# A decoder layer with a mixture of experts: two chunks of the shared expert's second half ahead of the expert blocks, six register loads inside them

## The chip, the core and the metric

The kernel runs on one core of a Trainium2 chip. Its engines are PE (TensorE), DVE (VectorE), ACT (ScalarE), POOL (GpSimd) and SP (SyncE, which here only issues DMAs). Each engine works its own instructions in order, and semaphores tie them together. The metric is the device time of one launch in microseconds (us).

## What is computed

One decoder layer on 8 sequences of 128 tokens with 256 features: self-attention, cross-attention, then a feed-forward part. The change touches only that last part:

```python
shared = _silu_and_mul(x @ shared_gate_up_w.T) @ shared_down_w.T      # 704 hidden features
shared = shared * jax.nn.sigmoid(x @ sgate_w.T)
router_logits = x @ gate_w.T                                          # 16 experts
topk_w, topk_ids = jax.lax.top_k(jax.nn.softmax(router_logits), TOP_K)   # TOP_K = 4
def body(acc, ew):
    w13_e, w2_e, e = ew
    coef = jnp.sum(jnp.where(topk_ids == e, topk_w, 0.0), axis=-1)
    h = _silu_and_mul(x @ w13_e.T)                                    # 176 hidden features
    return acc + (h @ w2_e.T) * coef[:, None], None
out = shared + sparse_out
```

The result is added to x.

## The kernel before, in words

Every engine's program is written out by hand; nothing is scheduled by a planner. After the attention the feed-forward part runs in three stages.

**First shared half.** The shared expert works on 1024 tokens in two halves of 512. Its 704 hidden features are cut into SC = 6 chunks, so there are chunks 0 to 5 for the first half and 6 to 11 for the second. Each chunk is one `rows_of(n)` on PE (12 matmuls into two banks: first the gate part, then the up part), a Silu on ACT (`gate`, L735), a product on DVE (`gated`, which writes `hid`, L1179), a rounded copy on ACT (`high_hidden`, `hid_h`, L742), the remainder on DVE (`low_hidden`, `hid_l`, L1184) and one `down(n)` on PE (6 matmuls into `ps_y`). All shared matmuls stand on one line, L1453. Buffers of `silu`, `hid`, `hid_h` and `hid_l` are double, by n % 2. After `down(5)` the sum is copied out (`y_t`, ACT `take_y` L747 and DVE `finish` L1190), transposed by `turn_rows` (PE L1641) and added to x by `add_shared` (DVE L1198).

**Expert blocks.** The tokens were scattered by expert into `x_slots` in DRAM (POOL L543). NBLK = 40 blocks of 128 rows follow, each with 64 rows of one expert ("even") and 64 of another ("odd"). POOL gathers a block's rows (`xb`, L605), PE transposes them (`turn_block`, L1703), ACT copies the result (`take_rows_t`, `xbt`, L781), PE multiplies by the expert's weights (`block_up`, L1713 and L1715), ACT and DVE make the hidden rows (`sg` L789, `hb` L1252), PE transposes them (`turn_hidden`, L1725), ACT copies (`hbt`, L796), PE multiplies (`block_down`, L1735 and L1737), DVE scales (`take_block`, `yb`, L1259) and POOL scatters to `y_picks` (L597). ACT also copies the odd expert's weights aside (`copy_up`, `w13_odd`, shown as `w_odd<-w`, L810). Which expert a block has is read from seven packed words (six blocks each). ACT reads its seven with register loads at L800 before its first `copy_up`; PE reads its seven at L1683, between `turn_rows` and `turn_block(0)`, and unpacks a block's number with `unpack` (L1690 to L1692).

**Second shared half.** After the blocks PE runs chunks 6 to 11 with `rows_of` one chunk ahead of `down`. Meanwhile the picked rows come back (`yg`, eight DMAs by SP, L455), and DVE adds them up in 24 steps (`combine`, L1288, L1290, L1292: three per sequence), dealt between the chunks' products. Then `finish(1)`, `turn_rows(1, ...)`, the four last additions (L1311) and the stores of x.

An instruction whose semaphore is not there yet stops everything behind it on its engine.

Of the kernel before, what the change touches and what calls it, by code (L numbers as in the profile page):

```python
# [17 lines left out]
B, T, D = 8, 128, 256  # L18
# [10 lines left out]
NE, HE, HS = 16, 176, 704  # L29
SC = -(-HS // 128)  # L30
# [26 lines left out]
WARM = (13, 3, 22, 3)  # L57


def decoder_layer(nc, x_in, ctx_in, ctxt_in, wqkv_in, bqkv_in, wo_in, bo_in, rope_in, masks_in, gate_in,  # L60
                  w13_in, w2_in, shared_in, ident_in, iota_in, tri_in, upto_in, picks_in, dump_in, packs_in, out):
    ctx = ExitStack()
    with ctx:
# [558 lines left out]
        def _(act):  # L622
# [147 lines left out]
            for n in range(3, SC):  # L770
                high_hidden(n)
                if n + 1 < SC:
                    gate(n + 1)
            take_y(0)

# [54 lines left out]
            gate(SC)  # L830
            for n in range(SC, 2 * SC):
                high_hidden(n)
                if n + 1 < 2 * SC:
                    gate(n + 1)
# [4 lines left out]
        def _(dve):  # L839
# [402 lines left out]
            dve.memset(hb[:, :, HE:D], 0.0).then_inc(hb_padded, 1)  # L1242
            finish(0)
            for pair in range(2):
                add_shared(0, pair)

# [52 lines left out]
            gated(SC)  # L1299
            for n in range(SC, 2 * SC):  # L1300
                low_hidden(n)
                if n + 1 < 2 * SC:
                    gated(n + 1)
                combine(5 * (n - SC), min(5 * (n - SC) + 5, 3 * B))
            finish(1)
            for pair in range(2):
                m = 2 + pair
                dve.wait_ge(rows_turned, m + 1)
                for i in range(2):
                    b = 2 * m + i  # L1310
                    dve.scalar_tensor_tensor(x2[:, b, :], ps_rows[pair][:, D * i:D * i + D], sig[:, b:b + 1], x2[:, b, :],  # L1311
                                             ALU.mult, ALU.add).then_inc(x_out_ready, 1)
# [3 lines left out]
        def _(pe):  # L1316
# [361 lines left out]
            block_table()  # L1678
            down(5)
            pe.wait_ge(table_ready, 2)  # L1680
            for pair in range(2):
                turn_rows(0, pair)
            packed = [pe.value_load(words[0:1, i:i + 1], min_val=0, max_val=NE ** PACK - 1) for i in range(WORDS)]  # L1683
# [9 lines left out]

            unpack(0)
# [46 lines left out]
            pe.wait_ge(hid_ready, SC)  # L1741
# [7 lines left out]
            for n in range(NBLK):  # L1749
                if n + 1 < NBLK:  # L1750
                    block_up(n + 1)
                if n + 2 < NBLK:
                    unpack(n + 2)
# [9 lines left out]
            rows_of(SC)  # L1763
            pe.wait_ge(hbt_ready, NBLK)
            for n in range(SC, 2 * SC):
                if n + 1 < 2 * SC:
                    rows_of(n + 1)
                down(n)
            pe.wait_ge(yb_ready, NBLK)
# [81 lines left out]
```

## Time and profile before

| | |
|---|---|
| median of 3 runs | 402.47 us (400.6 to 404.37) |
| profiled execution, device time | 401.02 us |
| its span, first to last instruction | 399.2 us |
| mean granted TensorE clock | 0.952 |
| PE busy | 340.4 us (85%) |
| PE weight loads busy | 214.2 us (54%) |
| DVE busy | 228.8 us (57%) |
| ACT busy | 207.0 us (52%) |
| POOL busy | 178.2 us (45%) |

Times in the rows are us from the start of the span. Shares of busy time are averages over stages: the attention runs to about 190, the first shared half to about 222, the blocks from about 227 to 365, and the rest is the second shared half. A granted clock of 1.00 is TensorE at 2.4 GHz, 0.50 is 1.2 GHz.

### The profile page before, as it was taken

What the parts mean: (1) busy time and instruction counts of PE and PEld (TensorE: products, weight loads), DVE (VectorE), ACT (ScalarE), POOL (GpSimd) and SP (SyncE); (2) the same over time, 40 slices, a digit from 0 to 9 for tenths busy, and PEclk for the clock granted to TensorE, in tenths of its full rate; (3) what the DMA queues carried; (4) which work ended last, traced back from release to release, by engine and by line L of the source; (5) the groups of instructions that cost most, each with busy time, mean ns of one, the idle gap of its engine ahead of it and who ended that gap; (6) DMA issues with size and microseconds to landing.
All of it is one profiled execution on the core that took longest, in us unless ns stands there. A gap on an engine that the chain in (4) does not pass through costs nothing.

```text
span 399.2 us, 7934 instructions
## 1 busy us (share of the span) xinstructions
PE 340.4 (85%) x2362; PEld 214.2 (54%) x2378; DVE 228.8 (57%) x688; ACT 207.0 (52%) x557; POOL 178.2 (45%) x212
## 2 busy tenths in 40 slices
PE   6988799999999986679699497888878978989993
PEld 2445376767667653567487243444443433446772
DVE  3286579889898797734356242433333423343884
ACT  1265578897898668553152264545354535452321
POOL 5481314354443434572475335555645555643000
PEclk9899699999999999958989799999989999999999
DMA  6997987779698661121492425545535544553931
GB/s 227 317 296 246 383 242 186 226 192 315 191 265 238 181 182 54 62 90 57 160 398 71 148 68 163 151 147 152 185 114 162 160 136 151 164 161 100 351 123 53
DMA packets 41747, 72.54 MB, mean 182 GB/s; under 512 B 5346, under 2 KB 29042, under 8 KB 40562
## 3 DMA queue, kind: packets, MB, share of 16 engines
q1 hardware_dynamic: 35490, 56.08, 45.8%
q0 software_dynamic: 5376, 15.13, 11.3%
q10 hardware_dynamic: 848, 0.92, 0.7%
q8 instruction: 17, 0.28, 0.3%
q14 instruction: 16, 0.13, 0.1%
HBM read 40.58 MB, written 31.53 MB: 181 GB/s over the span
## 4 chain that ended last, share of the span: by engine, by line
PE 44%; DVE 15%; issue 13%; ACT 9%; POOL 7%; another core or an unknown queue 6%; DMA 4%; ACTq 0%; POOLq 0%; DVEq 0%; SPq 0%
PE bank L1713 10%; ACT probs L650 6%; PE bank L1453 6%; PE bank L1735 5%; PE bank L1375 3%; DVE neg_max L911 3%; POOL x_slots L543 3%; PE bank L1725 3%; PE bank L1367 2%; PE bank L1331 2%; PE bank L1362 2%; PE bank L1423 2%; PE bank L1703 2%; PE bank L1396 2%
## 5 line engine op out<-in xcount | busy, mean ns | idle before, releaser
L650 ACT ACTIVATE probs<-bank,neg_max 128x128 f32<-128x128 f32 x256 | 70.1, 416 | 8.0 <-DVE neg_max L911 8.0
L1713 PE MATMUL bank<-w,xbt 128*64 x160 | 56.7, 480 | 19.5 <-ACT xbt L781 11.4
L597 POOL DMA_INDIRECT y_picks<-yb,ids x40 | 39.4, 985 | 49.9 <-DVE yb L1259 40.2
L1715 PE MATMUL bank<-w_odd,xbt 128*64 128x352 f32 x160 | 56.8, 481 | 0.0
L1252 DVE TENSOR_TENSOR hb<-sg,bank 128x176 f32<-128x176 f32 x40 | 13.5, 338 | 73.6 <-ACT sg L789 37.9
L605 POOL DMA_INDIRECT xb<-x_slots,rows x40 | 38.6, 964 | 20.0 <-issue 7.3
L789 ACT ACTIVATE sg<-bank 128x176 f32<-128x176 f32 x40 | 12.7, 318 | 65.9 <-PE bank L1715 45.4
L1713 PEld LDWEIGHTS bank<-w,xbt 128*64 128x64 f32 x160 | 21.2, 141 | 44.0 <-issue 36.0
L543 POOL DMA_INDIRECT x_slots<-x,slots x32 | 32.2, 1007 | 27.7 <-DVE slots L1040 19.2
L911 DVE TENSOR_REDUCE neg_max<-bank 128x4 f32<-128x512 f32 x64 | 41.4, 682 | 5.0 <-PE bank L1367 4.9
L1737 PE MATMUL bank<-w_odd,hbt 128*64 128x256 f32 x160 | 43.7, 397 | 0.0
L1735 PE MATMUL bank<-w,hbt 128*64 x160 | 43.7, 397 | 0.0
L1375 PE MATMUL bank<-ident,probs 128*128 128x128 f32 x256 | 38.4, 279 | 4.9 <-ACT probs L650 4.4
L1375 PEld LDWEIGHTS bank<-ident,probs 128*128 128x128 f32 x256 | 28.4, 141 | 12.1 <-ACT probs L650 11.7
L810 ACT ACTIVATE w_odd<-w 128x704 f32 x40 | 31.6, 793 | 4.3 <-issue 4.3
L1259 DVE TENSOR_SCALAR yb<-bank,offset 128x256 f32<-128x256 f32 x40 | 19.3, 484 | 15.6 <-PE bank L1737 12.9
L515 POOL TENSOR_TENSOR rstd<-ve,expo 128x1 f32<-128x1 f32 x16 | 9.3, 580 | 41.3 <-DVE ve L952 41.3
L1735 PEld LDWEIGHTS bank<-w,hbt 128*64 128x64 f32 x160 | 18.9, 138 | 13.0 <-issue 7.4
L917 DVE COPY probs_t<-bank 128x512 f32<-128x512 f32 x32 | 20.6, 682 | 5.1 <-PE bank L1375 5.0
L1715 PEld LDWEIGHTS bank<-w_odd,xbt 128*64 128x64 f32 x160 | 21.2, 141 | 0.0
L486 POOL TENSOR_TENSOR turned<-qkv,rope 128x320 f32<-128x320 f32 x8 | 6.9, 866 | 31.7 <-DVE qkv L872 31.7
L657 ACT ACTIVATE probs_t<-bank 128x512 f32<-128x512 f32 x32 | 18.6, 646 | 4.5 <-PE bank L1375 4.5
(181 smaller groups left out, 735.6 us busy)
## 6 DMA issues: line engine op xcount, KB each, us to landing
x_slots<-zero_b SPq DMA_DIRECT2D x16, 1072.0 KB, 10.5
w_odd<-w_in_dram SPq DMA_DIRECT2D x40, 256.0 KB
w<-w_in_dram SPq DMA_DIRECT2D x4, 1408.0 KB, 12.2
w<-w_in_dram SPq DMA_DIRECT2D x4, 1024.0 KB
yg<-y_picks SPq DMA_DIRECT2D x8, 512.0 KB, 7.0
ktc<-keys_d SPq DMA_DIRECT2D x16, 192.0 KB, 3.3
sw_raw<-shared_in_dram SPq DMA_DIRECT2D x6, 384.0 KB, 3.6
keys_d<-ctxt_h SPq DMA_DIRECT2D x4, 512.0 KB, 6.5
```

The lines of the kernel that those rows point to most:

```text
L543: pool.indirect_dma_start(x_slots[:, :], bass.IndirectOffsetOnAxis(slots[:, TOPK * b + k:TOPK * b + k + 1], 0), x[:, b, :], None).then_inc ...
L597: pool.indirect_dma_start(y_picks[:, :], bass.IndirectOffsetOnAxis(ids[:, n:n + 1], 0), yb[:, n % RB, :], None).then_inc(yb_placed[n % RB] ...
L605: pool.indirect_dma_start(xb[:, n % RB, :], None, x_slots[:, :], bass.IndirectOffsetOnAxis(rows[:, n:n + 1], 0)).then_inc(xb_loaded[n % RB ...
L650: ins = act.activation(probs[:, g, j, :], ps_s[g][:, 128 * j:128 * j + 128], ACT.Exp, bias=neg_max[:, g, j:j + 1])
L810: act.activation(w13_odd[:, n % 2, :, :], w13[:, bass.ds(e, 1), :, :].rearrange("p e k n -> p (e k) n"), ACT.Copy).then_inc(w13_odd_ready, 1)
L911: dve.tensor_reduce(neg_max[:, g, :], ps_s[g].rearrange("p (j n) -> p j n", j=BLK), AX.X, ALU.max, negate=True).then_inc(max_ready[kind], 1)
L1375: ins = pe.transpose(ps_s[g][:, 128 * j:128 * j + 128], probs[:, g, j, :], ident[:, :])
L1453: ins = pe.matmul(outs, w, m, start=first and i == 0, stop=last and i == len(todo) - 1, skip_group_check=not (first and last))
L1713: pe.matmul(ps_gu[n % 2][0:ROWS, 0:GU], xbt[:, n % 2, k, 0:ROWS], w13[:, bass.ds(experts[n], 1), k, :].rearrange("p e n -> p (e n)"), star ...
L1715: ins = pe.matmul(ps_gu[n % 2][ROWS:128, 0:GU], xbt[:, n % 2, k, ROWS:128], w13_odd[:, n % 2, k, :], start=k == 0, stop=k == KC - 1)
L1735: pe.matmul(ps_yb[n % 2][0:ROWS, 0:D], hbt[:, n % 2, k, 0:ROWS], w2[:, bass.ds(experts[n], 1), k, :].rearrange("p e n -> p (e n)"), start= ...
L1737: ins = pe.matmul(ps_yb[n % 2][ROWS:128, 0:D], hbt[:, n % 2, k, ROWS:128], w2_odd[:, n % RW, k, :], start=k == 0, stop=k == KC - 1)
```

## The change

`AHEAD = 2`: chunks 6 and 7 of the shared expert (SC and SC + 1) get their `rows_of`, Silu, product, rounded copy and remainder before the blocks; their `down` stays behind the blocks. On PE, `rows_of(SC)` stands ahead of `down(5)` and `rows_of(SC + 1)` behind it. Behind the blocks PE alternates `down(n)` with `rows_of(n + 2)`. PE loads one packed word before the blocks and one more in each of the blocks 0, 5, 10, 15, 20 and 25, behind `block_up(n + 1)`. ACT keeps its seven loads in one piece. The 24 additions of routed rows on DVE are dealt as 5, 6, 6, 0 behind four chunks, then 3, `finish(1)`, and 4; before they were dealt as 5, 5, 5, 5, 4, 0 behind six. The first block's transposes on PE now wait for the product of chunk 7 (`hid_ready`, SC + AHEAD).

```diff
@@ ACT
             for n in range(3, SC):
                 high_hidden(n)
-                if n + 1 < SC:
-                    gate(n + 1)
+                gate(n + 1)
             take_y(0)
+            high_hidden(SC)
+            gate(SC + 1)
+            high_hidden(SC + 1)
...
-            gate(SC)
-            for n in range(SC, 2 * SC):
+            for n in range(SC + AHEAD, 2 * SC):
+                gate(n)
                 high_hidden(n)
-                if n + 1 < 2 * SC:
-                    gate(n + 1)
             take_y(1)
@@ DVE
+            gated(SC)
             finish(0)
+            low_hidden(SC)
+            gated(SC + 1)
             for pair in range(2):
                 add_shared(0, pair)
+            low_hidden(SC + 1)
...
             dve.wait_ge(rows_added, HB)
-            gated(SC)
-            for n in range(SC, 2 * SC):
+            done = 0
+            for n, more in zip(range(SC + AHEAD, 2 * SC), (5, 6, 6, 0)):
+                gated(n)
                 low_hidden(n)
-                if n + 1 < 2 * SC:
-                    gated(n + 1)
-                combine(5 * (n - SC), min(5 * (n - SC) + 5, 3 * B))
+                combine(done, done + more)
+                done += more
+            combine(done, done + 3)
             finish(1)
+            combine(done + 3, 3 * B)
@@ PE
             block_table()
+            rows_of(SC)
             down(5)
+            rows_of(SC + 1)
             pe.wait_ge(table_ready, 2)
             for pair in range(2):
                 turn_rows(0, pair)
-            packed = [pe.value_load(words[0:1, i:i + 1], min_val=0, max_val=NE ** PACK - 1) for i in range(WORDS)]
+            packed = []
+
+            def load_word():
+
+                w = len(packed)
+                if w < WORDS:
+                    packed.append(pe.value_load(words[0:1, w:w + 1], min_val=0, max_val=NE ** PACK - 1))
...
+            load_word()
             unpack(0)
             unpack(1)
...
-            pe.wait_ge(hid_ready, SC)
+            pe.wait_ge(hid_ready, SC + AHEAD)
...
             for n in range(NBLK):
                 if n + 1 < NBLK:
                     block_up(n + 1)
+                if n % (PACK - 1) == 0:
+                    load_word()
                 if n + 2 < NBLK:
                     unpack(n + 2)
...
-            rows_of(SC)
             pe.wait_ge(hbt_ready, NBLK)
             for n in range(SC, 2 * SC):
-                if n + 1 < 2 * SC:
-                    rows_of(n + 1)
                 down(n)
+                if n + AHEAD < 2 * SC:
+                    rows_of(n + AHEAD)
```

Where the instructions stand now. First ACT, from the last rounded copy of the first half to its first register loads. `silu` is the Silu, `hid_h` the rounded copy, `y_t` the shared sum, `words` the packed expert numbers. Before:

```order
L742 ACTIVATE hid_h<-hid 128x512 [waits down_done,hid_ready]
L747 ACTIVATE y_t<-bank 128x512 [waits down_done]
L800 TENSOR_LOAD words [waits table_ready]
L800 ISA x2
L800 TENSOR_LOAD words
```

and now:

```order
L743 ACTIVATE hid_h<-hid 128x512 [waits down_done,hid_ready]
L736 ACTIVATE silu<-bank 128x512 [waits hid_ready,up_psum]
L748 ACTIVATE y_t<-bank 128x512 [waits down_done]
L743 ACTIVATE hid_h<-hid 128x512 [waits down_done,hid_ready]
L736 ACTIVATE silu<-bank 128x512 [waits hid_ready,up_psum]
L743 ACTIVATE hid_h<-hid 128x512 [waits down_done,hid_ready]
L803 TENSOR_LOAD words [waits table_ready]
L803 ISA x2
```

Two Silus and two rounded copies stand ahead of the seven loads; the loads themselves, the first two `copy_up` and the first two `xbt` follow in the old order.

Then PE in block 0, from the second `block_up` to the transpose of the first hidden rows. `w_109` are the even expert's weights, `w_odd` the odd one's. Before:

```order
L1713 MATMUL bank<-w_109,xbt 64x352
L1715 MATMUL bank<-w_odd,xbt 64x352
L1690 REGISTER_ALU
L1691 REGISTER_ALU
L1725 MATMUL bank<-ident,hb 128x128 [waits hb_ready]
```

and now:

```order
L1729 MATMUL bank<-w_109,xbt 64x352
L1731 MATMUL bank<-w_odd,xbt 64x352
L1698 TENSOR_LOAD words
L1698 ISA x2
L1706 REGISTER_ALU
L1707 REGISTER_ALU
L1741 MATMUL bank<-ident,hb 128x128 [waits hb_ready]
```

One load and its two register instructions have come between a block's matmuls and the next transpose, in six of the forty blocks.

## Rows read from the trace of the kernel before

**Rows 1.** Busy time by stretch: engines, then PE clock, DMA share, GB/s.

```profile
219.60:225.90 6.30, 1.06 (x8) 0.86 (x8) 2.34 (x5) 2.05 (x3) 3.46 (x4) 0.86 0.63 193
...
231.30:365.00 133.70, 114.18 (x785) 57.08 (x781) 49.61 (x195) 62.91 (x154) 72.33 (x75) 0.99 0.49 147
```

**Rows 2.** Chain that ended last, 221 to 226 us: start, length, what.

```profile
221.52 3.54 DMA xb<-x_slots,rows
225.06 0.89 issue
```

**Rows 3.** Timeline, 217 to 228 us: start, length, engine, line, what [idle before].

```profile
217.89 0.50 PE L1453 MATMUL bank<-hid_h,sw_h 128*128 128x512 f32 x1
...
219.59 0.60 ACT L747 ACTIVATE y_t<-bank 128x512 f32<-128x512 f32 x1 [3.21 <-issue]
...
220.43 1.06 PE L1641 MATMUL bank<-ident,y_t 128*128 128x128 f32 x8 [0.88 <-DVE y_t L1190]
...
224.04 1.47 ACT L810 ACTIVATE w_odd<-w 128x704 f32 x2 [3.85 <-issue]
...
226.66 0.38 ACT L781 ACTIVATE xbt<-bank 128x256 f32<-128x256 f32 x1 [1.15 <-issue]
...
227.19 0.84 PE L1713 MATMUL bank<-w,xbt 128*64 x1
```

**Rows 4.** Register loads of ACT (L800) and PE (L1683): ns, first and last start.

```profile
L800 ACTq TENSOR_LOAD <-words x7: 273/275/651, 219.6 to 223.2; - x7
...
L1683 PEldq TENSOR_LOAD <-words x7: 301/304/495, 220.5 to 224.6; - x7
```

**Rows 5.** Timeline behind the blocks: one chunk of the second half.

```profile
364.94 0.73 PE L1453 MATMUL bank<-xth,sw_h 128*128 128x512 f32 x2
...
368.15 0.69 DVE L1179 TENSOR_TENSOR hid<-silu,bank 128x512 f32<-128x512 f32 x1 [2.61 <-PE bank L1453]
...
368.87 0.63 ACT L742 ACTIVATE hid_h<-hid 128x512 fp32r<-128x512 f32 x1 [1.64 <-DVE hid L1179]
...
369.53 0.69 DVE L1184 TENSOR_TENSOR hid_l<-hid,hid_h 128x512 fp32r<-128x512 f32 x1 [0.70 <-ACT hid_h L742]
...
370.51 0.40 PE L1453 MATMUL bank<-hid_h,sw_h 128*128 128x512 f32 x1
...
370.77 0.69 DVE L1179 TENSOR_TENSOR hid<-silu,bank 128x512 f32<-128x512 f32 x1 [0.54 <-PE bank L1453]
...
371.91 0.63 PE L1453 MATMUL bank<-xth,sw_h 128*128 128x512 f32 x2
```

**Rows 6.** Block 37 on PE: last register instruction of `unpack`, then the transpose.

```profile
L1692 PEldq MOVE  x1: 29/29/29, 357.5 to 357.5; - x1
...
L1725 PE MATMUL bank<-ident,hb x2: 273/300/328, 358.4 to 358.6; 128*128 128x128 f32 x2
```

**Rows 7.** Busy time by shorter stretches, columns as in rows 1.

```profile
199.80:204.00 4.20, 4.17 (x13) 3.34 (x14) 2.81 (x5) 2.65 (x6) 3.37 (x4) 0.59 1.01 422
...
230.00:231.00 1.00, 1.00 (x6) 0.48 (x4) 0.67 (x4) 0.70 (x2) 0.00 (x0) 0.51 0.00 0
```

**Rows 8.** Timeline of the second half's end.

```profile
372.20 0.69 DVE L1288 TENSOR_TENSOR yg<-yg 128x512 f32<-128x512 f32 x1 [0.74 <-DMA yg<-y_picks]
...
374.90 0.69 DVE L1184 TENSOR_TENSOR hid_l<-hid,hid_h 128x512 fp32r<-128x512 f32 x1
...
391.90 0.51 PE L1453 MATMUL bank<-hid_h,sw_h 128*128 128x512 f32 x1 [1.77 <-DVE hid_l L1184]
...
393.60 0.69 DVE L1190 COPY y_t<-bank 128x512 f32<-128x512 f32 x1 [1.76 <-PE bank L1453]
...
395.10 1.66 DVE L1311 SCALAR_TENSOR_TENSOR x<-bank,sig,x 128x256 f32<-128x256 f32 x4 [0.81 <-PE bank L1641]
```

**Rows 9.** Waits in the blocks, 226 to 364 us: us in total, times, longest.

```profile
ACT sg L789 <- PE bank L1715: 45.4, 33, 2.3
...
ACT sg L789 <- remote: 19.6, 6, 4.2
```

More of the change, by code:

```diff
@@ L57 @@
 WARM = (13, 3, 22, 3)
+AHEAD = 2
 def decoder_layer(nc, x_in, ctx_in, ctxt_in, wqkv_in, bqkv_in, wo_in, bo_in, rope_in, masks_in, gate_in,
```

## The prediction

> **What bounds the kernel now.** I read the busy time by stretch first. Of the places that the change touches it has a stretch of 6.3 us before the blocks in which PE is busy for only 1.06, and the blocks themselves (133.7 us, PE busy 114.2) [rows 1]. The change moves two chunks' worth of PE work from behind the blocks into the first stretch.
>
> Next the chain across the gap. It runs over the first gather (221.52, landed at 225.06) and 0.89 of issue to the first transposes on PE [rows 2]. So PE's hole belongs to a DMA, and PE work put there looks free. But the chain shows only the wait that ended last. The timeline shows a second one nearly as long on ACT: after `y_t` at 219.59 ACT does nothing until `copy_up` at 224.04, and its first `xbt` follows at 226.66; `block_up(0)` starts at 227.19 [rows 3]. The register loads fill that hole: seven on ACT with starts from 219.6 to 223.2, 0.6 each, and seven on PE from 220.5 to 224.6, (224.6 - 220.5) / 6 = 0.68 each [rows 4]. PE's loads begin while its `turn_rows` matmuls (220.43 for 1.06) still run, so a load needs PE's sequencer and not its array [rows 3, 4].
>
> ACT has little slack there: the two `copy_up` end at 224.04 + 1.47 = 225.51, `xbt` starts at 226.66. That is 1.15 us [rows 3].
>
> **Term 1, the start of the blocks.** Prices of a chunk come from behind the blocks: two `rows_of` take 364.94 to 370.51, so 2.78 each; a `down` takes 370.51 to 371.91, 1.40; the product of chunk 7 starts at 370.77, which is 3.05 after its `rows_of` (364.94 + 2.78 = 367.72); the rounded copy starts 368.87 - 368.15 = 0.72 after a product, the remainder 369.53 - 368.15 = 1.38 after it [rows 5].
>
> PE used to start `down(5)` at 217.89 [rows 3]. Now `rows_of(6)` runs from 217.89 to 220.67, `down(5)` to 222.07, `rows_of(7)` to 224.85. The product of chunk 7 starts at 222.07 + 3.05 = 225.12, its rounded copy on ACT at 225.84. DVE and ACT are free by then: `y_t` starts 1.70 after `down(5)` does (219.59 - 217.89), at 220.67 + 1.70 = 222.37, and chunk 6's rounded copy and remainder behind it end by 224.4.
>
> ACT's seven loads stand behind that rounded copy. Before, ACT's first `copy_up` came 224.04 - 219.59 = 4.45 after the activation ahead of the loads began; now it comes at 225.84 + 4.45 = 230.29. Two copies (1.47) bring `xbt(0)` to 231.76 instead of 226.66, and `block_up(0)` to 232.29. **That is +5.1 us**, though the gather lands at 225.06 as before. SP, POOL and their queues are passed by nothing, since they are not touched. PE's own six loads that leave this place save nothing, because ACT's seven end later than the one PE keeps.
>
> Bounds: not below +3.9 (4.45 counted without ACT's first slow load, 0.65 instead of 0.28, and 0.8 off the chunk), not above +6.0 if `y_t` pushes chunk 6 and 7 back by one ACT copy and one DVE copy more.
>
> **Term 2, TensorE's clock.** The granted clock fell during PE's idle, was still 0.51 between 230 and 231, and is 0.99 on the mean from 231.3 on [rows 1, 7]. Block matmuls from 227.19 to about 231.2 thus ran at 1.2 GHz, 4.0 us for what takes 2.0. Now PE idles from about 226.5 (both `turn_block` done) to 232.29, 5.8 us, longer than the idle before, so I expect the fall again. The fall before that one, from 199.8 to 204.0 with 0.59 on the mean, was shorter: 4.2 x (1 - 0.59) / 0.5 = 3.4 us at half speed [rows 7]. Ends: -2.0 if the clock never falls, +1.0 if it stays low 2 us longer. I take -0.5, since the transposes at least no longer run slow.
>
> **Term 3, loads in the blocks.** Six loads of 0.68 are 4.1 us if PE stands still for each. The order puts each behind a block's matmuls were dispatched. In block 37 the sequencer was through with `unpack` at 357.5 while the transpose behind it started at 358.4: PE's sequencer is 0.9 ahead of the array there [rows 6]. A load of 0.68 fits. So I take 0, upper end 4.1, lower end 0 (a load gives nothing back).
>
> The Trainium skill, in "DMA: Bandwidth & Descriptors", section on latency and other measured facts, gives a register load a floor of about 600 ns; it speaks against this edit, because six would be an estimated 3.6 if none were hidden. By the row above the sum has 0 for them.
>
> **Term 4, the end.** I count u from PE's first shared matmul behind the blocks (364.94). Before, the last additions begin at u = 395.10 - 364.94 = 30.16 and the span ends 4.1 after that [rows 5, 8]. Now PE does `down(6)` to 1.40, `rows_of(8)` to 4.18, `down(7)` to 5.58, `rows_of(9)` to 8.36, and is ready to be done with all ups at 16.7. DVE decides. Product of chunk 8 at 1.40 + 3.05 = 4.45, remainder done at 4.45 + 1.38 + 0.69 = 6.52. The picked rows arrive at 372.20, u = 7.26, since nothing in their chain is touched; five steps take 372.20 to 374.90, 2.7, so six take 3.2 [rows 8]. Then:
> - five steps to 9.9, chunk 9 (product to remainder 2.07) to 12.0,
> - six steps to 15.2, chunk 10 to 17.3,
> - six steps to 20.5, chunk 11 to 22.6,
> - `down(11)` on PE, 1.70 until its copy (391.90 to 393.60 [rows 8]), 24.3; three steps beside it,
> - `finish(1)` to 25.0, four steps to 27.1; the transposes end at 25.8 in their shade,
> - last additions from 27.1 instead of 30.16: **-3.1 us**.
> Bounds: -1.5 (if each chunk's copy on ACT costs DVE 0.4 more) to -4.0.
>
> **Sum.** 5.1 - 0.5 + 0 - 3.1 = +1.5. Against the profiled execution, 401.02, that is 402.5. The median of the runs shown, 402.47, lies 1.45 above that execution, so as a median I write 402.47 + 1.5 = 404.0.
>
> **Rivals.**
> - *The clock stays up* because PE works through the old hole. Against it: the new hole is longer. 402.47 + 5.1 - 2.0 - 3.1 = 402.5. Chance 0.14.
> - *The loads in the blocks show.* For it: ACT waits for PE's `block_up` 33 times, 45.4 us, so PE is what the blocks wait for [rows 9], and 0.9 ahead is not much. 402.47 + 1.5 + 4.1 = 408.1. It decides from about 2.6 us exposed, 0.4 per load. Chance 0.17.
> - *The rhythm of the blocks shifts.* Six waits of ACT for something that the trace can't name took 19.6 us [rows 9]; one more or one less is 3.3, so 400.7 or 407.3. The three runs of before already lie 3.8 apart. Chance 0.13, both signs.
> - *Faster: the end becomes PE's.* If the additions fit beside PE's work, the end is 4 x 2.78 + 6 x 1.40 = 19.5, then 0.3, 1.5 to the additions: 21.3 instead of 30.16, -8.9, and 402.47 + 5.1 - 0.5 - 8.9 = 398.2. It needs DVE to be idle less than my list has it, from u = 7.3 on; DVE's list is solid there. Chance 0.06.
> - My forecast: 0.50, its own range 402 to 406.
>
> **How the numbers follow.** About 1% (4.0 us, 398.4 to 406.5) is what a measurement of this kernel can tell from no change. Faster by more: 0.06 and a part of the rhythm, 0.09. Slower by more: 0.17, a part of the rhythm and the top of term 1, 0.23. Same: 0.68. The range goes from the rhythm's lower case, 400.4, to the exposed loads, 408.0.
>
> **What would show it.** Right: `copy_up` starts at about 230, `block_up(0)` at about 232.3, ACT's register loads begin right behind a `hid_h` at 225.8; the last block ends about 4.6 later than before; from there to the end of the span 3.1 less. Wrong: `block_up(0)` before 230 (term 1), the first PE transpose of hidden rows in blocks 0, 5, 10 later after `block_up` than in their neighbours (term 3), DVE waiting for PE again behind u = 10 (term 4).

## The result, and the profile after

| | before | after |
|---|---|---|
| median, five executions of each side by side | 400.6 us (396.39 to 404.37) | 405.3 us (403.41 to 411.7) |
| ratio, 95% interval | | 1.0172 [1.0097, 1.0247] |
| profiled execution | 401.02 us | 409.17 us |
| its span | 399.2 us | 407.2 us |
| mean granted TensorE clock | 0.952 | 0.937 |
| product of chunk 5 to `block_up(0)` | 12.50 us | 17.36 us |
| `block_up(0)` to `block_up(5)` | 15.52 us | 16.48 us |
| `block_up(5)` to the end of the last block | 122.29 us | 121.90 us |
| end of the last block to the last additions | 30.09 us | 30.62 us |

The changed kernel is 4.7 us slower by the medians. Twelve more executions of it on a chip that also ran the kernel before gave 400.24 against 395.66, a ratio of 1.0119 [1.0074, 1.0165]. So the change costs between 1 and 2%, nearer 1. All ratios here leave out executions more than 1.5% above the fastest of the same kernel.

Its profiled execution is not a typical one: its span is 8.0 us longer, and 2.04 of that lies ahead of everything the change touches (the product of chunk 5 on DVE starts at 216.74, before at 214.70). The last four lines of the table hold the other 6.0: +4.86, +0.96, -0.39, +0.53. I use such stages for all runs below, each taken from the starts of the same instructions in the timeline.

First the start of the blocks, from the timeline of the changed kernel (start, length, engine, line, what, and in brackets the idle time ahead and what ended it), then its register loads by line (ns, first and last start):

```profile
219.97 0.73 PE L1460 MATMUL bank<-xth,sw_h 128*128 128x512 f32 x2
...
222.83 0.40 PE L1460 MATMUL bank<-hid_h,sw_h 128*128 128x512 f32 x1
...
224.42 0.60 ACT L748 ACTIVATE y_t<-bank 128x512 f32<-128x512 f32 x1 [2.16 <-PE bank L1460]
...
227.94 0.63 ACT L743 ACTIVATE hid_h<-hid 128x512 fp32r<-128x512 f32 x1 [1.54 <-DVE hid L1180]
...
232.21 1.47 ACT L813 ACTIVATE w_odd<-w 128x704 f32 x2 [3.64 <-issue]
...
234.09 0.84 PE L1729 MATMUL bank<-w,xbt 128*64 x1 [4.70 <-ACT xbt L784]
```

```profile
L803 ACTq TENSOR_LOAD <-words x7: 272/275/471, 227.9 to 231.4; - x7
...
L1698 PEldq TENSOR_LOAD <-words x7: 297/308/493, 225.3 to 323.3; - x7
```

ACT's seven loads run from 227.9 on, behind the rounded copy of chunk 7, and leave ACT idle by the profile for 3.64. PE waits 4.70 for the `xbt` behind them. Before, the same wait on ACT stood right behind `y_t`, beside the gather [rows 3]. The second thing is the clock. Busy time by stretch of PE alone (length, PE busy, clock, DMA share, GB/s), first of the kernel before, then of the changed one:

```profile
223.00:224.00 1.00, 0.00 (x0) 1.00 0.84 272
224.00:225.00 1.00, 0.00 (x0) 0.58 0.89 266
```

```profile
232.00:233.00 1.00, 0.00 (x0) 1.00 0.00 0
233.00:234.00 1.00, 0.00 (x0) 0.66 0.02 8
...
239.00:240.00 1.00, 1.00 (x6) 0.50 0.00 0
240.00:241.00 1.00, 0.44 (x3) 0.92 0.47 116
```

In both kernels the clock fell to its lower level, 1.2 GHz, after PE had been idle (since 221.5 before, since 229.4 now), and stayed there for nearly 7 us (from about 224.2 to 231.0 [rows 7], and from 233.3 to 240.1). Before, 3.0 of these passed before `block_up(0)` at 227.19; now only 0.8 did, so 2.2 us more of block matmuls ran at half speed, an estimated 1.1; the stage is 0.96 longer.

Last the end of the changed kernel, where the picked rows `yg` come back. The last two lines are from the view of the DMAs between 376 and 385 us: `q8` holds instruction fetches, and the last number of the other line is the median time from issue to landing.

```profile
380.46 0.69 DVE L1293 TENSOR_TENSOR yg<-yg 128x512 f32<-128x512 f32 x1 [1.35 <-DMA yg<-y_picks]
...
383.85 0.69 DVE L1293 TENSOR_TENSOR yg<-yg 128x512 f32<-128x512 f32 x1 [1.78 <-DMA yg<-y_picks]
...
385.04 0.69 DVE L1180 TENSOR_TENSOR hid<-silu,bank 128x512 f32<-128x512 f32 x1
...
387.17 0.50 PE L1460 MATMUL bank<-hid_h,sw_h 128*128 128x512 f32 x1 [2.07 <-DVE hid_l L1185]
...
397.36 0.80 PE L1460 MATMUL bank<-hid_h,sw_h 128*128 128x512 f32 x1 [3.49 <-DVE hid_l L1185]
...
403.09 1.66 DVE L1318 SCALAR_TENSOR_TENSOR x<-bank,sig,x 128x256 f32<-128x256 f32 x4
```

```profile
q8 instruction: 1, 0.02, 1.0%
...
yg<-y_picks SPq DMA_DIRECT2D x8, 512.0 KB, 8.3
```

DVE's fourth addition waits 1.78 for the second block of rows, with the product of chunk 9 (385.04) queued behind it, and PE's `down(9)` behind that. The last `down` starts behind 3.49 of idle at half clock (0.80 for its first matmul, 0.50 at 387.17). Before, the second block of rows was taken 1.53 after the first (8.71 and 7.19 behind the last block); here 3.39 after it. "Behind the last block" means from the end of its last `block_down` here and below.

### The profile page after: what moved, and what is told of

Read it like the earlier page. It is cut to its first block, busy times and chain, and to the rows that moved or that the text cites. A ratio compares the mean times of both kernels' runs of the same rounds, so it can differ in the third digit from the quotient of the medians.

```text
span 407.2 us, 7933 instructions
## 1 busy us (share of the span) xinstructions
PE 343.3 (84%) x2362; PEld 217.9 (54%) x2378; DVE 227.9 (56%) x688; ACT 206.8 (51%) x557; POOL 178.6 (44%) x212
## 4 chain that ended last, share of the span: by engine, by line
PE 43%; DVE 15%; issue 12%; another core or an unknown queue 9%; ACT 9%; POOL 6%; DMA 3%; ACTq 1%; POOLq 0%; DVEq 0%; SPq 0%
PE bank L1460 10%; PE bank L1729 8%; ACT probs L651 5%; PE bank L1382 4%; DVE neg_max L912 3%; PE bank L1751 3%; PE bank L1338 2%; PE bank L1741 2%; PE bank L1374 2%; POOL x_slots L544 2%; DMA yg<-y_picks 2%; PE bank L1605 2%; PE bank L1430 2%; PE bank L1403 2%
## 5 line engine op out<-in xcount | busy, mean ns | idle before, releaser
L1382 PE MATMUL bank<-ident,probs 128*128 128x128 f32 x256 | 40.0, 288 | 4.8 <-ACT probs L651 4.4
L1382 PEld LDWEIGHTS bank<-ident,probs 128*128 128x128 f32 x256 | 30.3, 148 | 11.8 <-ACT probs L651 11.5
L743 ACT ACTIVATE hid_h<-hid 128x512 fp32r<-128x512 f32 x12 | 7.6, 630 | 31.4 <-DVE hid L1180 28.5
```

The costliest lines, as they stand in the source:

```text
L1382: ins = pe.transpose(ps_s[g][:, 128 * j:128 * j + 128], probs[:, g, j, :], ident[:, :])
```

## Experiments

All kernels of one group ran on the same chip with the kernel before; groups 2 and 3 shared one chip, on which the kernel before had a median of 395.66 in the first and 397.52 in the second. All stages come from one profiled execution of each kernel, the medians from 6 or 12 (the first group from 5, `r_before` from 2). "Taken" is when DVE starts on the first and second block of picked rows.

| kernel | group | median, of before | ratio, interval | chunk 5 to `block_up(0)` | blocks 0 to 5 | block 5 to end | taken, behind last block | last additions |
|---|---|---|---|---|---|---|---|---|
| before | first | 400.6 | | 12.50 | 15.52 | 122.29 | 7.19, 8.71 | 30.09 |
| changed | first | 405.3, 400.6 | 1.0172 [1.0097, 1.0247] | 17.36 | 16.48 | 121.90 | 7.98, 11.38 | 30.62 |
| words_only | 1 | 400.65, 400.81 | 1.0022 [0.9972, 1.0071] | 12.81 | 15.47 | 122.47 | 7.14, 8.67 | 30.06 |
| ahead_only | 1 | 402.39, 400.81 | 1.0055 [1.0011, 1.0098] | 17.38 | 16.45 | 121.58 | 7.39, 10.01 | 27.98 |
| act_words | 1 | 399.11, 400.81 | 0.9968 [0.9927, 1.0009] | 14.19 | 13.50 | 122.70 | 7.36, 10.23 | 29.45 |
| redeal | 1 | 403.99, 400.81 | 1.0068 [1.0023, 1.0113] | 16.47 | 16.10 | 126.41 | 9.14, 11.40 | 26.97 |
| r_after | 2 | 400.24, 395.66 | 1.0119 [1.0074, 1.0165] | 17.51 | 16.16 | 118.62 | 8.00, 9.69 | 27.68 |
| act_words_late | 2 | 392.69, 395.66 | 0.9893 [0.9832, 0.9953] | 12.24 | 13.53 | 117.90 | 7.99, 9.94 | 28.21 |
| best1 | 2 | 392.6, 395.66 | 0.9854 [0.9786, 0.9921] | 13.27 | 13.57 | 120.46 | 9.13, 11.39 | 26.95 |
| warm | 2 | 398.66, 395.66 | 1.0026 [0.9967, 1.0085] | 17.50 | 13.36 | 118.54 | 7.18, 8.71 | 27.93 |
| shift | 3 | 399.03, 397.52 | 1.0146 [1.0075, 1.0217] | 17.51 | 16.26 | 118.63 | 7.44, 8.96 | 28.19 |
| best2 | 3 | 392.92, 397.52 | 0.9966 [0.9894, 1.0039] | 12.22 | 13.60 | 117.89 | 7.37, 10.62 | 25.56 |
| before_act_words | 3 | 396.63, 397.52 | 1.0071 [1.0024, 1.0117] | 12.54 | 15.47 | 117.77 | 7.38, 8.91 | 31.48 |
| r_before | 3 | 397.1, 397.52 | 1.0105 [0.9984, 1.0227] | 12.22 | 15.02 | 117.88 | 7.37, 8.89 | 30.31 |

In group 3 I go by the medians: one of before's 23 executions stood alone at 390.06, and even the kernel before against itself, `r_before`, comes out at a ratio of 1.0105 there.

### The loads inside PE's blocks

The kernel before, with this part of the change alone:

```diff
-            packed = [pe.value_load(...) for i in range(WORDS)]
+            load_word()
...
                     block_up(n + 1)
+                if n % (PACK - 1) == 0:
+                    load_word()
```

> The kernel before with one part of the change alone: PE loads one packed word ahead of the blocks and six inside them. Theory (the loads inside the blocks are hidden, since PE's sequencer runs ahead of its array there; the change loses its time on ACT's seven loads, which this kernel leaves where they were): no change against the kernel before, within 1 us, and the transposes of hidden rows in blocks 0, 5, 10, 15, 20 and 25 come as soon behind block_up as in their neighbours. Rival 1 (the loads stop PE): six times 0.68 us, so 4.1 us slower than before, which would be nearly the whole of the loss of the changed kernel (405.3 against 400.6, 4.7). Rival 2 (taking six loads out of PE's path ahead of the blocks brings the blocks forward): at most 1 us faster, because ACT's first xbt comes at 226.66 and waits for nothing of PE's but the transposes.

```profile
L1689 PEldq TENSOR_LOAD <-words x7: 296/307/495, 219.6 to 316.8; - x7
```

One load lies ahead of the blocks, six inside them, the first at 227.61 and the next at 244.84. The time is that of before, 400.65 against 400.81, where rival 1 had 4.1 us. In blocks 0, 5, 10, 15, 20 and 25 the transpose starts 0.39 after the last matmul of `block_up` starts, exactly as in their neighbours. The loads are hidden.

The other half, the changed kernel with PE's seven loads left ahead of the blocks:

```diff
+            packed = [pe.value_load(...) for i in range(WORDS)]
...
-            load_word()
...
-                if n % (PACK - 1) == 0:
-                    load_word()
```

> The changed kernel with PE's seven loads all ahead of the blocks, as before the change, so chunks 6 and 7 ahead and the additions dealt anew are what is left of it. Theory (all of the loss is ACT's seven loads behind the rounded copy of chunk 7): as slow as the changed kernel, ratio 1.012 to 1.02 against the kernel before, block_up(0) at about 234 less the 2 us by which that profile was late ahead of the change, and copy_up about 4.3 us behind ACT's last rounded copy. Rival 1 (loads inside the blocks cost): 4.1 us faster than the changed kernel, about 401. Rival 2 (PE's seven loads behind the later turn_rows become the last thing that the blocks wait for): turn_block(0) about 0.3 us before PE's last load ends, and 1 to 3 us slower than the changed kernel.

Its timeline:

```profile
229.33 0.63 ACT L743 ACTIVATE hid_h<-hid 128x512 fp32r<-128x512 f32 x1 [1.54 <-DVE hid L1180]
233.60 1.47 ACT L813 ACTIVATE w_odd<-w 128x704 f32 x2 [3.65 <-issue]
```

```profile
235.49 0.84 PE L1722 MATMUL bank<-w,xbt 128*64 x1 [2.65 <-ACT xbt L784]
```

`copy_up` comes 4.27 behind the rounded copy, the same as in the changed kernel (232.21 - 227.94), and the start takes 17.38, the same too, so rival 2 falls. By the profile, then, the loss needs nothing but the chunks ahead. By its time the kernel stands at 1.0055, below the 1.012 that I expected and below the changed one's 1.0119, but that was on another chip and the intervals overlap; the times alone don't settle it. The stretch from block 5 on does, within one chip each: in group 1 with PE's loads 122.47 (`words_only`), without 121.58; in groups 2 and 3 with them 118.62 (`r_after`) and, with ACT's too, 117.77 (`before_act_words`), without 117.88 (`r_before`). That is -0.1 to 0.9 for six loads, where rival 1 has 4.1.

### ACT's loads

The changed kernel with ACT's loads dealt into the blocks:

```diff
-            packed = [act.value_load(...) for i in range(WORDS)]
+            load_word()
...
                 if n + 3 < NBLK:
+                    if (n + 3) // PACK >= len(packed):
+                        load_word()
                     copy_up(n + 3)
```

> The changed kernel with ACT's loads put inside the blocks too, one ahead and each other one right ahead of the first copy_up that needs it. Theory: six loads of about 0.53 us leave ACT's path ahead of the blocks, so copy_up comes 3 us sooner behind the last rounded copy (1.3 instead of 4.27) and block_up(0) with it; the kernel is about 3 us faster than the changed one, 402.3. Rival 1 (ACT's loads show inside the blocks, where ACT's sg is what block_down waits for): 3 us gained ahead, 3 us lost inside, 405.3, with sg later behind block_up in the blocks that hold a load. Rival 2 (something else than ACT's loads holds block_up(0), such as the clock or the gather): block_up(0) moves by less than 1 us.

Timeline of ACT and of PE, and the loads by line:

```profile
224.94 0.63 ACT L743 ACTIVATE hid_h<-hid 128x512 fp32r<-128x512 f32 x1 [1.54 <-DVE hid L1190]
226.02 1.47 ACT L821 ACTIVATE w_odd<-w 128x704 f32 x2 [0.44 <-issue]
227.40 0.64 ACT L784 ACTIVATE xbt<-bank 128x256 f32<-128x256 f32 x2
```

```profile
227.91 0.51 PE L1739 MATMUL bank<-w,xbt 128*64 x1 [1.65 <-ACT xbt L784]
```

```profile
L809 ACTq TENSOR_LOAD <-words x7: 274/278/471, 225.0 to 345.2; - x7
```

`copy_up` comes 1.08 behind the rounded copy, not 4.27, and the start takes 14.19, 3.2 less. PE now waits only 1.65, and the clock does not fall (PE alone, with the clock behind its busy time):

```profile
227.00:228.00 1.00, 0.10 (x2) 1.00 0.00 0
```

So blocks 0 to 5 take 13.50 instead of 16.48, another 3.0. By these stages the edit is worth 6 us, twice what I expected, since I had priced the loads without the clock. The times show less for certain. On the same chip, `ahead_only` is the changed kernel but for PE's hidden loads, and `act_words` is 3.3 us below it by the medians (399.11 against 402.39), which is what I expected; against the changed kernel on the other chip the ratios differ by 1.5% (0.9968 and 1.0119). Rival 2 falls. Rival 1, which has 3 us there, falls too: the stretch from block 5 on is 122.70, against 122.47 in `words_only` and 121.58 in `ahead_only`, and `before_act_words` below, with both engines' loads in it, has 117.77 against 117.88 without any.

With the rounded copy of chunk 7 also moved, behind the first two `xbt`:

```diff
             gate(SC + 1)
-            high_hidden(SC + 1)
...
             take_rows_t(1)
+            high_hidden(SC + 1)
             block_gate(0)
```

> The changed kernel with ACT's loads inside the blocks and, besides, the rounded copy of chunk 7 on ACT moved behind the first two xbt. Theory (ACT's list ahead of the first xbt is what holds the blocks): copy_up follows one load behind the Silu of chunk 7, xbt(0) is held by copy_up or by the first transposes on PE, and block_up(0) comes 4 to 5 us sooner behind y_t than in the changed kernel (9.68), so 5 to 5.7; the kernel is 1 us faster than the one with the loads moved alone, about 398 where before is 400.8. Rival (PE's down(5) and rows_of(7) are then the bound: turn_block(0) waits for the product of chunk 7): block_up(0) 6.0 to 6.5 behind y_t, as with the loads moved alone (6.48), and no difference between the two.

Timeline of ACT and of the first transposes on PE:

```profile
219.34 0.60 ACT L736 ACTIVATE silu<-bank 128x512 f32<-128x512 f32 x1 [0.26 <-PE bank L1470]
220.42 1.47 ACT L820 ACTIVATE w_odd<-w 128x704 f32 x2 [0.48 <-issue]
222.16 0.41 PE L1729 MATMUL bank<-ident,xb 128*128 128x128 f32 x2 [0.62 <-DMA xb<-x_slots,rows]
222.61 0.38 ACT L783 ACTIVATE xbt<-bank 128x256 f32<-128x256 f32 x1 [0.72 <-issue]
```

`xbt(0)` is now held by the gather and the transposes, and `block_up(0)` follows `y_t` by 5.44, where the changed kernel needs 9.68 and `act_words` 6.48, as expected. The start, 12.24, is nearly as short as in the old order with two chunks of the shared expert done in it. It has to be compared like with like: in four of the fourteen profiles (`r_before`, `redeal`, `act_words_late`, `best2`) `y_t` stands about 1 us nearer to the product of chunk 5 (4.04 instead of 4.9 to 5.0 in the old order, 6.80 instead of 7.7 to 7.8 in the new). Since the kernel before does so too, this is not the change. Among these four the start takes 12.22 in the old order and 12.24 and 12.22 in this one (here and in `best2`); among the others 12.50 to 12.81 in the old order, and 13.27 in this one (`best1`). The kernel is 1.1% faster than the kernel before.

Whether that comes from the loads alone is asked by the kernel before with both engines' loads inside the blocks:

> The kernel before with both engines' loads inside the blocks and no chunk ahead. It asks whether the gain over before comes from the loads alone. Theory (in the kernel before the loads lie in the shade of the first gather, which landed at 225.06, 1.2 us ahead of xbt(0) less the transposes): xbt(0) comes at most 1 us sooner, the time is within 1 us of before, ratio 0.997 to 1.002, and running two chunks ahead is what makes the rest. Rival (ACT's loads were the bound already): 3 us faster, ratio 0.992, in which case the chunks ahead add little over it.

Medians 396.63 and 397.52, start 12.54, clock low as before (blocks 0 to 5 in 15.47). The theory holds by these: in the old order the loads lay beside the gather and cost nothing. The ratio, 1.0071, is above the range that I expected, in the group in which `r_before` has 1.0105; no time shows a gain.

### The clock

```diff
             turn_block(1)
+            keep_clock(18)
             block_up(0)
```

> The changed kernel with 18 matmuls on zeros added on PE between turn_block(1) and block_up(0), into the hole of about 5 us in which PE waits for ACT. Theory (the hole costs the clock on top of the wait): the granted clock stays 1.00 through the first two block_up, which then take 1.4 us each instead of 2.6, so the blocks run 2 us sooner from there and the kernel is 1.5 to 2 us faster than the changed one. Rival 1 (the first blocks wait for weights and gathered rows anyway): block_up(0) and (1) take 1.4, block_up(2) starts no sooner, and the time does not change. Rival 2 (the matmuls last into ACT's xbt): block_up(0) up to 1 us later. A second thing is told by the same run: in the four profiles with chunks ahead an instruction fetch falls 3.5 to 3.8 us behind the last block, together with the issue of the picked rows' loads, and the second block of picked rows arrives 10 to 11.4 behind it instead of 8.7 or less. The added instructions move that fetch earlier by about one block. If the fetch is what slows the rows, they arrive by 8.7 here; if not, at 10 or later again.

Timeline of PE, then busy time by stretch (PE, PE's weight loads, DVE, ACT, POOL, clock, DMA share, GB/s):

```profile
225.71 4.05 PE L1605 MATMUL bank<-zero_b 128*128 128x512 bf16 x18
230.98 0.51 PE L1729 MATMUL bank<-w,xbt 128*64 x1 [1.23 <-ACT xbt L784]
```

```profile
231.00:235.00 4.00, 3.38 (x22) 1.69 (x24) 1.59 (x8) 2.56 (x7) 0.54 (x1) 1.00 0.02 4
```

The start is as late as in the changed kernel (17.50), the clock stays up, and blocks 0 to 5 take 13.36 instead of 16.16 to 16.48. The ratio falls from 1.0119 to 1.0026 and the median by 1.6 us. So by the stages the hole costs 2.8 to 3.1 us in clock on top of its length, and the times agree with that (1.6 us by the medians, an estimated 3.7 by the ratios); rival 1 falls.

### The end

Products and remainders of chunks 8 and 9 ahead of all additions:

```diff
-            for n, more in zip(range(SC + AHEAD, 2 * SC), (5, 6, 6, 0)):
+            for n, gap, more in zip(range(SC + AHEAD, 2 * SC), (0, 1, 1, 1), (0, 4, 4, 3)):
                 gated(n)
+                combine(done, done + gap)
                 low_hidden(n)
-                combine(done, done + more)
-                done += more
-            combine(done, done + 3)
+                combine(done + gap, done + gap + more)
+                done += gap + more
             finish(1)
-            combine(done + 3, 3 * B)
+            combine(done, 3 * B)
```

> The changed kernel with DVE's order behind the blocks dealt anew and nothing else: products and remainders of chunks 8 and 9 stand ahead of all additions, one addition fills the wait between product and remainder of chunks 9, 10 and 11, four more follow chunk 9, four chunk 10, three chunk 11, and the other ten finish(1). Theory (the end gained nothing because the additions stood ahead of chunk 9's product, and DVE waited there for the second block of picked rows, 1.78 us in the changed kernel's profile, with PE's down(9) behind it, idle for 2.07): PE waits less than 0.5 us ahead of down(9), the last additions begin 27 to 28 us after PE's first shared matmul behind the blocks instead of 30.7, and the kernel is 2.5 to 3.5 us faster than the changed one, about 402. Rival (the end is set by DVE's own work or by the picked rows whatever the order): the last additions stay at 30 to 31, and the time within 1 us of the changed kernel's.

```profile
381.11 0.69 DVE L1180 TENSOR_TENSOR hid<-silu,bank 128x512 f32<-128x512 f32 x1 [1.95 <-PE bank L1460]
381.71 0.68 DVE L1293 TENSOR_TENSOR yg<-yg 128x512 f32<-128x512 f32 x1
...
399.53 1.66 DVE L1318 SCALAR_TENSOR_TENSOR x<-bank,sig,x 128x256 f32<-128x256 f32 x4
```

The product of chunk 9 comes as soon as PE has it, and the last additions start at 399.53 - 372.56 = 26.97 behind the last block, as expected, and at 26.95 in `best1`, which has the same deal. The time did not show it: 403.99 is the median of twelve, 1.6 above `ahead_only` on the same chip, where I had expected some 3 us less. In the one execution that was profiled the blocks took 142.5 us in all, over 4 more than any other of its group, and the trace says where most of that lies (block 5 to the end on PE, first here, then in `ahead_only`):

```profile
246.14:372.57 126.43, 108.67 (x717) 0.95 0.49 146
251.95:373.53 121.58, 102.47 (x717) 1.00 0.51 151
```

The same matmuls kept PE busy for 6.2 us more, because the granted clock fell four times inside the blocks, for some 13 us in all, and never in `ahead_only`. What made it fall there is not known, nor whether it did in the other eleven. The place of the additions is right by the profile and unproved by the time of this run.

The changed kernel again:

> The changed kernel again, unaltered, beside the kernel before, for twelve more executions and a second profile. Theory: the blocks start 4.8 us later for ACT's loads, the loads inside PE's blocks cost nothing, and the end gives back 0.5 to 2 (the last additions begin 28 to 30.6 us behind the last block instead of 30.1), so 3 to 4.5 us slower than before, a ratio of 1.007 to 1.011, the same as the kernel that has only chunks 6 and 7 ahead (1.0055 with its interval up to 1.0098). The 1.0172 of the first five executions would then be in part chance, since their profile came 2.1 us late already ahead of the change. Rival (the loads inside PE's blocks cost, or cost through something that one profile does not show): ratio 1.015 or more, that is 4 us slower than the kernel with only the chunks ahead.

```profile
371.14 0.69 DVE L1293 TENSOR_TENSOR yg<-yg 128x512 f32<-128x512 f32 x1 [1.37 <-DMA yg<-y_picks]
...
372.82 0.69 DVE L1293 TENSOR_TENSOR yg<-yg 128x512 f32<-128x512 f32 x1
373.55 0.43 DVE L1295 TENSOR_TENSOR yg<-yg 128x256 f32<-128x256 f32 x1
374.01 0.69 DVE L1180 TENSOR_TENSOR hid<-silu,bank 128x512 f32<-128x512 f32 x1
```

```profile
386.32 0.50 PE L1460 MATMUL bank<-hid_h,sw_h 128*128 128x512 f32 x1 [3.47 <-DVE hid_l L1185]
```

Here the second block of rows came 1.68 after the first, the last `down` ran at full clock (0.50), and the last additions came at 27.68. So the end of the first profile, 30.62, was a bad one, by about 1.7 for the rows and 1.3 for the clock. The start (17.51) and blocks 0 to 5 (16.16) are nearly the same as there. It is 4.6 us slower than before by the medians (ratio 1.0119), just above what I expected.

What makes the rows late? In all seven profiles so far that have chunks ahead and no added matmuls, an instruction fetch starts 3.5 to 3.8 behind the last block, together with SP's issue of the rows. In `warm`, whose PE program is longer, the fetch came at 0.6 and the rows at 7.18 and 8.71. The test changes only where instructions lie in PE's program:

```diff
             keep_clock(WARM[0])
+            for _ in range(18):
+                pe.matmul(ps_s[0][:, 0:16], zero_b[:, 0:128], zero_b[:, 0:16], start=True, stop=True)
```

> The changed kernel with 18 tiny matmuls (16 columns each, on zeros) added at the very start of PE's program, where PE waits 2.6 us anyway. They move every later instruction of PE in its program by the same amount and do nothing else. Theory (where PE's instruction fetches fall decides when the picked rows arrive): in the four profiles with chunks ahead and the old additions an instruction fetch starts 3.5 to 3.8 us behind the last block and the second block of rows is taken 9.7 to 11.4 behind it; in the one whose PE program was 18 matmuls longer ahead of the blocks the fetch came at 0.6 and the rows were taken at 8.7, as in the kernel before. Here then: fetch at about 0.6, first addition at 7.2, the second block of rows at 8.7 with no wait ahead of it, last additions at 26.5 to 28 instead of 27.7 to 30.6, and the kernel 0 to 1.5 us faster than the changed one (ratio against before 1.005 to 1.012). Rival (it is the clock or the blocks' end that decides, and the one profile was chance): second block of rows at 9.7 or later.

Timeline of DVE:

```profile
372.04 0.69 DVE L1293 TENSOR_TENSOR yg<-yg 128x512 f32<-128x512 f32 x1 [0.80 <-DMA yg<-y_picks]
...
373.57 0.68 DVE L1293 TENSOR_TENSOR yg<-yg 128x512 f32<-128x512 f32 x1
```

And SP's second load of rows, with how long its issue took (ns) and its time to landing, in `r_after` and then in `shift`:

```profile
L456 SPq DMA_DIRECT2D yg<-y_picks x1: 1238/1238/1238, 367.2 to 367.2; - x1
DMA to landing us min/median/max: 5.6/5.6/5.6
...
L456 SPq DMA_DIRECT2D yg<-y_picks x1: 426/426/426, 368.7 to 368.7; - x1
DMA to landing us min/median/max: 4.6/4.6/4.6
```

The fetch started 0.2 behind the last block and the second block of rows was taken 1.52 after the first, with no wait between. The second load is the clearest sign: with the fetch beside it, it landed 5.1 to 7.3 us after its issue in seven profiles, without it 4.4 to 4.6 in the other seven. (The median over all eight loads is not: 7.4 both in `r_after` and in `warm`.) Chunk 9's product stands at 10.14 instead of 10.88 and 12.56. The last additions came at 28.19 all the same, just above what I expected, since the clock fell ahead of the last `down` as in the first profile. So the fetch delays the rows, which the runs show; that a lower clock costs the last `down` about 1.3 is shown as well, but nothing here shows what decides whether it falls there. By the medians it is 1.5 above before, where the changed kernel in group 2 was 4.6; the ratio says otherwise, and the time of this run settles nothing.

### Put together

`best1` has ACT's loads inside the blocks, the late rounded copy and the new deal.

> ACT's loads inside the blocks, the rounded copy of chunk 7 behind the first xbt, and the additions dealt anew behind chunks 8 and 9, together. Theory (the three places are independent, since they lie before, inside and behind the blocks): block_up(0) as early as with the first two, last additions 27.0 behind the last block as with the third (26.97 there), so 4 us off the end of the changed kernel's profile (30.6) and 3 off that of before (30.1): about 395, ratio 0.985 to 0.99 against the kernel before. Rival (the blocks' own rhythm, 136.2 to 142.5 us in six profiles, takes back what is gained ahead of them, since the gathers and weights come when they come): ratio 0.995 or more.

`best2` has in addition the 18 tiny matmuls and two additions between chunks 8 and 9.

> ACT's loads inside the blocks, the rounded copy of chunk 7 behind the first xbt, the 18 tiny matmuls at the start of PE's program, and the additions dealt as 2 behind chunk 8, then one between product and remainder of chunks 9, 10 and 11, with 4, 4 and 3 behind them, and 8 behind finish(1). Theory: the rows arrive by 8.7 behind the last block, so two additions fit ahead of chunk 9's product and the last additions begin at about 26 instead of 26.95 without that; ratio 0.98 to 0.985 against the kernel before. Rival 1 (the two additions delay chunk 9's product, which stood at 8.5, and PE with it): last additions at 27 or later. Rival 2 (the rhythm of the blocks hides 1 us): ratio as without it, 0.985.

```profile
361.99 0.69 DVE L1303 TENSOR_TENSOR yg<-yg 128x512 f32<-128x512 f32 x1 [0.80 <-DMA yg<-y_picks]
362.72 0.42 DVE L1305 TENSOR_TENSOR yg<-yg 128x256 f32<-128x256 f32 x1
363.25 0.69 DVE L1190 TENSOR_TENSOR hid<-silu,bank 128x512 f32<-128x512 f32 x1
...
380.18 1.66 DVE L1330 SCALAR_TENSOR_TENSOR x<-bank,sig,x 128x256 f32<-128x256 f32 x4
```

`best1` is 1.5% faster than the kernel before by the ratio and 0.8% by the medians, against 1.1% and 0.8% for `act_words_late`: the new deal's 1.3 us at the end can't be told from nothing in the times. `best2` brings the last additions to 380.18 - 354.62 = 25.56, and chunk 9's product at 8.62 is hardly later than in `best1` (8.53). Its median is 4.6 us below that of before, 1.2%; its ratio, 0.9966, misses the 0.98 to 0.985 that I expected, in the group whose ratios are not to be trusted. These three kernels beat the kernel before by about 1% and the changed one by about 2%; which of them is best stays open.

And the kernel before again:

> The kernel before again, unaltered, for one more profile of it on the chip that runs the others. Theory: from the product of chunk 5 to block_up(0) 12.5 us (17.4 in the changed kernel), the last additions 30.1 behind the last block with the second block of picked rows taken at 8.7, as in its first profile; the blocks between them anywhere from 131 to 138, as the other profiles. Rival (the end of the kernel before varies as that of the changed kernel does, 27.7 to 30.6): more than 0.5 away from 30.1.

Start 12.22, last additions 30.31, rows at 7.37 and 8.89, as expected. What runs from block 5 on takes 117.88 here and 122.29 in the first profile: that stage is the largest source of difference between executions and chips, and the change does not show in it (118.62 and 121.90 with it).

## Why the prediction came out as it did

The range, 400.4 to 408.0, held the time (405.3), and the sum was 1.3 below it. (The lower end should read 400.7, 404.0 - 3.3.) Part of this is luck: I counted from a median of 402.47, and beside the changed kernel the kernel before measured 400.6. As a change, the forecast was +1.5 and the medians give +4.7 and +4.6. The class I thought likeliest, within 1%, was not what came.

- **Term 1, +5.1.** Right: +4.9 in the first pair of profiles (17.36 against 12.50). The second pair, 17.51 against 12.22, gives 5.3, but `r_before` is one of the four profiles with an early `y_t`; against the old order's other three (12.50 to 12.81) it is 4.7 to 5.0. Each step is there: `rows_of(6)` to `y_t` 4.45 after 4.48 expected, 4.27 from the rounded copy to `copy_up` after 4.45, and `act_words` gives 3.2 back when six of the loads go.
- **Term 2, -0.5.** Wrong in sign: blocks 0 to 5 take 16.1 to 16.5 in the changed order and 15.0 to 15.5 in the old one, +0.9 on the means, +0.96 and +1.14 in the two pairs. I saw that the clock would fall again, but took the 3.4 us from an earlier, shorter fall and did not ask how much of the low stretch lies in the hole itself. The kernel before had let 3.0 of nearly 7 us pass there (`r_before` 3.8, with the shortest stage, 15.02); now 0.8 pass. The bound of +1.0 just held the mean.
- **Term 3, 0.** Right: `words_only` and the stretch from block 5 on. The lead of 0.9 us that I read from one block was enough for a load of 0.68. The floor of about 600 ns a load, from the Trainium skill, "DMA: Bandwidth & Descriptors", section on latency and other measured facts, is near the spacing of the loads (0.68 on PE; 0.57 on ACT, where those behind the first stand 0.53 apart, so below it), but on this path none of it showed.
- **Term 4, -3.1.** The mechanism is there, the size is not. Seven profiles with the changed deal have the last additions at 27.68 to 30.62, 28.6 on the mean; those of the old order at 30.06 to 31.48, 30.5 on the mean: -1.9. That lies inside my bounds; the first profile alone, +0.5, lies far outside. The step that failed is "The picked rows arrive at 372.20, u = 7.26, since nothing in their chain is touched", with the five steps counted from there at full pace. The first block came at 7.2 to 8.0, the second up to 1.9 later than the five steps want it, and these steps now stand ahead of chunk 9's product. The rest is the clock at the last `down`, which I priced at full speed (1.70; it was 400.39 - 397.36 = 3.03 where the clock had fallen, the first number being the start of DVE's `y_t`). Where neither happens my list holds: chunk 9's product, which I had at 9.9, came at 9.89 in `warm`, and the last additions, 6.6 behind chunk 11's product by the list, came 6.62 behind it in `r_after` and `ahead_only`.
- **The sum.** With what the stages measured, 4.9 + 0.9 + 0 - 1.9 = +3.9; the medians give +4.6 and +4.7. The 0.7 left is less than these measurements can tell.
- **The rivals.** The clock stayed up: no, but `warm` shows that it would have been worth 3 us, not 2. Loads in the blocks: no. Rhythm: the blocks' time differs from execution to execution whatever the kernel, and no run shows a shift by the change. The end becomes PE's: no, it gave 1.9 and not 8.9. The chance for slower by over 1% was 0.23, and it should have come from terms 2 and 4 together, which I had not let err in the same direction.

## What to carry to other kernels

Work moved into one engine's idle time pushes back whatever stands behind it on the engines that help with it. Here PE's hole was free, but ACT's register loads stood behind the two chunks' copies, and moving these loads and the rounded copy ahead of them (not the chunks) turned a loss of 1.2% into a gain of 1%; the loads alone brought it to no loss (0.9968, with 1 inside its interval). When a hole moves, ask where the low clock that follows it will lie: what passes inside the hole is free, as the 3.0 us here were. Before additions that wait for a DMA are put ahead of a product that the bound engine needs, ask what happens if the DMA is 2 us late.

## What the runs showed of the hardware that was not expected

- An instruction fetch of PE's (0.02 MB on its own queue, `q8`) that starts together with the loads of the picked rows makes them late: the second of eight blocks of 512 KB was taken 1.7, 1.9, 2.6, 2.9 and 3.4 us after the first in the five profiles where it did and the order of the additions lets it be seen, and 1.5 in the six where it did not. SP's own issue of the second load took longer too (1.24 us in `r_after`, 0.43 in `shift`). Tiny matmuls elsewhere in the program move the fetch.
- Once fallen, the granted clock stayed at 1.2 GHz for nearly 7 us in the kernel before (224.2 to 231.0) and in the changed one (233.3 to 240.1), though PE was busy through the last 6 of these in the latter.
- Register loads that take 0.57 (ACT, 227.94 to 231.37 for six steps) and 0.68 us each (PE) back to back cost nothing measurable inside the blocks on either engine.
